# Encoder queries: the exponential clipped on GpSimd, the map fed from PSUM, no lifted copy on ScalarE

## The reference

```python
def _phi(t):
    return jax.nn.elu(t) + 1.0
# for each of 8 layers, for each sequence h [256, 128]:
#   q, k = _phi(h @ Wq + bq), _phi(h @ Wk + bk);  v = h @ Wv + bv
#   linear attention with 16 heads: state = k^T v per head, att = (q state) / (q sum(k) + 1e-6)
#   h1 = LN(h + att @ Wo + bo);  h = LN(h1 + gelu(h1 @ W1 + c1) @ W2 + c2)
```

## Time and profile before

| | us |
|---|---|
| median of three runs | 2956.65 (2946.87 to 2959.39) |
| the profiled execution | 2955.58 |
| its span in the trace | 2954.2 |
| TensorE busy | 2508.7 (85%) |
| VectorE busy | 2083.3 (71%) |
| ScalarE busy | 1787.4 (61%) |
| GpSimd busy | 1189.5 (40%) |

### The profile page before, as it was taken

How to read it: one execution, slowest core, us unless ns; L and a number is a source line. 1 busy time by engine, 2 the same in 40 slices (tenths; PEclk the granted TensorE clock), 3 DMA queues, 4 the chain that set the end, 5 groups by cost and what they waited for, 6 DMA issues and landing times.

```text
span 2954.2 us, 67889 instructions
## 1 busy us (share of the span) xinstructions
PE 2508.7 (85%) x25429; PEld 1981.5 (67%) x25429; DVE 2083.3 (71%) x7733; ACT 1787.4 (61%) x3496; POOL 1189.5 (40%) x1634
## 2 busy tenths in 40 slices
PE   7799998768599769459689999999999998895886
PEld 4467775446477547336479899999988996563555
DVE  6667765873377844664378888888888888546877
ACT  5444445434255334336369999999989996563553
POOL 4200002575623557565542332322234433556413
PEclk9899998979799879679789999999999999997997
DMA  9910000014300024225300000000010100441001
GB/s 233 279 43 3 3 3 1 9 47 137 91 26 26 30 76 137 80 87 160 108 19 16 19 21 14 21 14 14 14 34 23 37 23 8 127 153 36 24 3 30
DMA packets 149543, 164.59 MB, mean 56 GB/s; under 512 B 15713, under 2 KB 123874, under 8 KB 149218
## 3 DMA queue, kind: packets, MB, share of 16 engines
q1 hardware_dynamic: 120770, 85.53, 10.9%
q0 software_dynamic: 28448, 74.71, 8.2%
HBM read 85.18 MB, written 75.01 MB: 54 GB/s over the span
## 4 chain that ended last, share of the span: by engine, by line
PE 38%; DVE 13%; POOL 4%; issue 3%; ACT 1%; DMA 1%; DVEq 0%; POOLq 0%; ACTq 0%
PE banks L3570 6%; PE banks L3555 6%; PE banks L3500 3%; POOL bins L3212 2%; PE banks L3517 2%; PE banks L3536 2%; PE banks L3509 2%; PE banks L3493 1%; PE banks L3535 1%; PE banks L3247 1%; PE banks L3258 1%; PE banks L3260 1%; PE banks L3248 1%; PE banks L3249 1%; PE banks L3526 1%
## 5 line engine op out<-in xcount | busy, mean ns | idle before, releaser
L3671 POOL TENSOR_SCALAR shared_floats<-shared_floats 128x2 f32<-128x2 f32 x256 | 57.7, 225 | 582.7 <-DVE shared_floats L3662 579.0
L3570 PE MATMUL banks<-layer,shared_floats 128*128 128x128 f32 x2048 | 292.0, 275 | 0.0
L3570 PEld LDWEIGHTS banks<-layer,shared_floats 128*128 128x128 f32 x2048 | 258.8, 192 | 0.0
L3555 PE MATMUL banks<-shared_floats,layer 128*128 128x256 f32 x1024 | 243.9, 381 | 0.0
L3960 ACT ACTIVATE shared_floats<-banks,layer 128x256 f32<-128x256 f32 x512 | 210.3, 471 | 51.0 <-PE banks L3555 51.0
L3555 PEld LDWEIGHTS banks<-shared_floats,layer 128*128 128x128 f32 x1024 | 185.9, 192 | 20.2
L3673 POOL TENSOR_TENSOR shared_floats<-shared_floats,neg_half 128x2 f32<-128x2 f32 x256 | 183.7, 717 | 21.3
L1395 POOL DMA_INDIRECT results<-shared_floats,e_token_rows x160 | 155.3, 971 | 89.4 <-issue 48.2
L3683 DVE TENSOR_SCALAR shared_floats<-banks,shared_floats 128x128 f32<-128x128 f32 x512 | 185.4, 403 | 7.3 <-POOL shared_floats L3673 7.3
L2164 DVE TENSOR_REDUCE shared_floats<-banks 128x2 f32<-128x512 f32 (+3 forms) x256 | 110.5, 484 | 91.2 <-PE banks L2028 89.7
L256 PE MATMUL banks<-ident,xn 128*128 128x128 f32 x320 | 60.4, 320 | 133.4 <-issue 82.3
(11 more groups left out here) (444 smaller groups left out, 7939.3 us busy)
## 6 DMA issues: line engine op xcount, KB each, us to landing
bins<-zero SPq DMA_DIRECT2D x1, 18176.0 KB, 69.3
layer<-in_dram_layers SPq DMA_DIRECT2D x16, 902.0 KB, 4.6
bins<-layer SPq DMA_DIRECT2D x16, 650.0 KB, 13.2
shared_floats<-bins SPq DMA_DIRECT2D x32, 325.0 KB, 3.5
expert_weights<-in_dram_experts SPq DMA_DIRECT2D x32, 312.0 KB, 3.1
results<-results SPq DMA_DIRECT2D x32, 256.0 KB, 3.3
results<-zero SPq DMA_DIRECT2D x1, 4096.0 KB, 16.1
bins<-xn,f_bin_row POOLq DMA_INDIRECT x256, 2.3
```

Source lines behind the costliest of these rows:

```text
L3555: m = T.matmul(k.bank[5 + half][:, part], w["w1"][:, tile(n)], h1[:, :], start=True, stop=True)
L3570: m = T.matmul(to, hidden[:, n * S + t * P:n * S + (t + 1) * P], w["w2"][:, tile(n)], start=False, stop=(n == NF - 1), skip_group_check=True)
```

## The change

ScalarE no longer makes the lifted copy (lift_q, e2_q_plus). Its exponential of the queries, exps_q, takes over the waits. GpSimd gets a new instruction per unit, clip_q, which takes the smaller of the exponential and 1 in place, and which stands first in GpSimd's step. VectorE's map_q now reads bank 0, adds (bias + 1) and takes the larger of that and the clipped exponential; it waits for GpSimd. map_k comes before map_q now, and map_q carries the semaphore e2_qk, so that it stands for both. As bank 0 is now read until the end of map_q, TensorE's waits before bank 0 is written again (project_q and all the extra work) are on e2_qk, not on the exponential. In the second half of narrow one product stands ahead of turn_att and three behind it, where it was two and two.

```diff
@@ project_q, and leave in the same way
         if u:
-            T.wait_ge(k.sem("e2_exp_q"), u)
+            T.wait_ge(k.sem("e2_qk"), u)
         T.matmul(k.bank[0][:, LOW], w["wq"], h, start=True, stop=True).then_inc(k.sem("e2_q_made"), 1)
@@ TensorE's step
-            narrow(g - 3, 1, 0, NF // 2)
+            narrow(g - 3, 1, 0, 1)
         if 1 <= g <= U2:
             turn_att(g - 1)
         if g in TURNING:
-            T.wait_ge(k.sem("e2_exp_q"), g + 1)
+            T.wait_ge(k.sem("e2_qk"), g + 1)
             ln_turn(k, s, TURNING[g])
...
         if s.next and (g in ROWS_TURN_AT or g in GATES_AT or g in COUNT_AT):
-            T.wait_ge(k.sem("e2_exp_q"), g + 1)
+            T.wait_ge(k.sem("e2_qk"), g + 1)
...
-            narrow(g - 3, 1, NF // 2, NF)
+            narrow(g - 3, 1, 1, NF)
@@ VectorE
     def map_q(u):
-        q, exp_q, q1 = (k.sb(n, [P, S]) for n in (f"e2_q{u % 2}", "e2_exp_q", "e2_q_plus"))
-        V.wait_ge(k.sem("e2_exp_q"), u + 1)
-        v.count(V.scalar_tensor_tensor(out=q[:, :], in0=exp_q[:, :], scalar=1.0, in1=q1[:, :], op0=ALU.min, op1=ALU.max))
+        q, exp_q = k.sb(f"e2_q{u % 2}", [P, S]), k.sb("e2_exp_q", [P, S])
+        V.wait_ge(k.sem("e2_clipped"), u + 1)
+        V.scalar_tensor_tensor(out=q[:, :], in0=k.bank[0][:, LOW], scalar=layer_weights(k, u)["bq1"], in1=exp_q[:, :],
+                               op0=ALU.add, op1=ALU.max).then_inc(k.sem("e2_qk"), 1)
...
         if g < U2:
+            map_k(g)
             map_q(g)
-            map_k(g)
@@ ScalarE
-    def lift_q(u):
-        w, q1 = layer_weights(k, u), k.sb("e2_q_plus", [P, S])
...
-        a.count(A.activation(q1[:, :], k.bank[0][:, LOW], ACT.Identity, bias=w["bq1"]))
...
-        A.activation(exp_q[:, :], k.bank[0][:, LOW], ACT.Exp, bias=w["bq"]).then_inc(k.sem("e2_exp_q"), 1)
+        A.activation(exp_q[:, :], k.bank[0][:, LOW], ACT.Exp, bias=w["bq"]).then_inc(k.sem("e2_exps"), 1)
@@ GpSimd
+    def clip_q(u):
+        exp_q = k.sb("e2_exp_q", [P, S])
+        G.wait_ge(k.sem("e2_exps"), 2 * u + 1)
+        G.tensor_scalar(exp_q[:, :], exp_q[:, :], 1.0, None, ALU.min).then_inc(k.sem("e2_clipped"), 1)
...
     for g in range(STEPS2):
+        if g < U2:
+            clip_q(g)
         if TURNING.get(g + 1, NC) not in (*ONE_BY_ONE, NC):
```

## The result

The changed kernel takes **2987.0 us** (median of four runs, 2983.8 to 2990.3) where the kernel before takes 2955.2 in the same comparison: a ratio of 1.0115, 95% interval 1.0097 to 1.0132, so 1.15% slower. The forecast was 2975 and the range 2952 to 2992. The profiled execution is 2983.84 us, its span 2982.4, which is 28.2 above the span before.

What follows compares the result with a forecast made beforehand. TensorE was taken to bound the encoder's long middle, VectorE and in places GpSimd's queue its ends. 2955.6 - 13.4 (plain steps) + 1 (VectorE-limited steps) + 18.9 (bank 0 waits) + 6.5 + 6.4 (queue) = 2975 us; range 2952 to 2992.

Steps and rivals of the forecast that it cites:

- The plain step: Encoder steps without extra turning, TensorE-limited: attention copy 0.16 us sooner, 7.52 to 7.36; 84 steps, 13.4 us gained (0 to 17.6).
- The clip: GpSimd's new instruction on 128x256 in SBUF: 0.40 us taken, bounds 0.31 and 0.76, plus 0.05 for the wait.
- if the clip takes over 0.65, as it then delays every step: Sign against the forecast: a GpSimd clip longer than 0.65 us would delay all steps.
- Part 2: Clip of 0.40 us covered in plain steps, 0.25 to spare before VectorE asks; 1 us lost for all VectorE-limited steps.
- The waits for bank 0: Steps using bank 0 for extra work: TensorE now waits for VectorE's queries' map; 27 x 0.70 = 18.9 us lost (13 to 23).
- turning step: Encoder step in which TensorE also transposes a residual chunk, such as step 29: 8.4 us forecast instead of 7.73.
- GpSimd's queue: Clip behind queued gathers, scatters and roots: 6.5 us lost at the start, 6.4 in steps 88, 96, 104 and 112.
- Part 4: Pricing of clips late in GpSimd's in-order queue: steps 0 and 1 lose 6.5 us, four late steps 1.6 each.
- The turning waits are empty: Rival: TensorE meets no wait for VectorE's queries' map in steps turning a chunk; 2956 us, not slower; chance 0.20.
- the plain steps gain nothing: Rival: in steps without extra turning, slight lateness of VectorE's division eats the gain; 2989 us; chance 0.14.
- The queue does not bite: Rival: no loss from GpSimd's queue, bank 0 waits cost 0.35 each, whole 0.21 gained; 2947 us, faster; chance 0.09.
- the second rival: Same as "the plain steps gain nothing": 2989 us in the text, chance 0.14.

## Why the prediction was right, and where it was off

The direction, the places of the main terms and their signs were right, and 2987 lies inside the range; the sum was 12 too low by the medians, and by its own terms 14 (33.6 against 19.4), of which 5.4 is hidden again, by chance, by the stretch outside the encoder. The largest error was the price of the clip, and one place of loss was missed.

- **The plain step: right in mechanism, 0.06 short in size.** Forecast 7.36, measured 7.30; the whole 0.21 went. "From there ScalarE runs without a gap to the attention copy" was the weak step: copy_att needn't wait for the full 0.55 of copy_h1; it starts 0.45 to 0.48 behind copy_h1's start when its input is there. That the two edits only work together was argued there and is shown by the four kernels: a plain step falls by nothing with the copy left out, by 0.11 with the product moved and by 0.22 with both. The number of plain steps was 84 in the text; 67 gained the 0.22 from widening to widening (63 by the mark of the table, which hides the gain of 30, 46 and 62 and some others in the step ahead of each). That the sums come out alike, 13.4 forecast and 13.6 or 14.7 measured, is luck: the count was too high and the gain per step too low. Of the other 17, six (25, 27, 41, 43, 57, 59) come behind steps in which VectorE has spare work between map_q and the statistics (24, 26 and so on); there the clip comes too late, and they rose by 0.08 to 0.18 instead of falling. With the clip of 0.55 us they fell by 0.04 to 0.11. 26 and 119 gained less, 0.15 and 0.09. 83, 91, 99, 107 and 115 gained 0.13 to 0.14; that the mark shows them 1.14 longer is its fault again, as by the widenings the wait for bank 0 lies in 82, 90 and so on, 1.05 each, where the text had put it. 78, 79 and 80 rose, by 0.21, 0.93 and 0.10, and 23, 9.12 long before, stayed.
- **The clip: the mis-sized term.** 0.40 taken, 0.76 as the upper end, 0.87 measured. Both nearest rows were too cheap a guide: the copy of 128x512 in rows 6 takes 611 ns, and an operation of one input and half the columns takes 260 ns more. By one of its own signs the prediction would be wrong: "if the clip takes over 0.65, as it then delays every step". That sign did not hold: at 0.87 the 67 plain steps still gained their 0.22, and a clip that ends 1.46 behind its start costs a plain step 0.24. The 0.65 is the 0.40 and the 0.25 to spare before VectorE asks; Part 2 itself had the statistics behind map_q wait for TensorE for another 0.22, and the sign left that room out.
- **The waits for bank 0: right in mechanism, too small with the clip.** Priced 0.70, so that a turning step would take 8.4; from widening to widening step 29 took 8.85, 1.12 more than before, and most of the late borrowing steps lost 1.00 to 1.06. The 0.90 by the mark of the table has the gain of step 30 in it. By the clip of 128 columns 0.34 of the 1.12 is the clip's length, and 0.78 stays with a shorter clip, as map_q comes last on VectorE and its end, not the exponential's, releases TensorE. So the 0.70 was near for the clip it was worked out with, and the 0.85 for a clip of 0.76 was some 0.15 too low (1.12 less the 0.11 by which that clip is shorter). In eight late steps (85, 89 and every four to 113) 0.22 to 0.24 of the loss is the moved product, which the kernel with neither copy nor clip loses too; the text had it in its price for step 89, 0.50 + 0.22.
- **GpSimd's queue: right in place, too small.** VectorE's wait in step 0 was to be 6 us and was 7.10; in step 1 it was to be 6 again and was 1.79. Part 4's own sum does not give 6 there: it has VectorE 4.85 late already when the map of step 1 comes 6.3 late, which leaves about 1.5 of wait. In step 88 it was 3.26 where 2.5 was forecast; the 0.47 by which the clip is longer makes most of that. Missed altogether were five clips (steps 78, 86, 94, 102, 110) that stand behind the 1.04 us root of a leaving chunk; the steps behind them (79, 87, 95, 103, 111) lost 0.9 each. What Part 4 lists ahead of the clip are gathers, scatters and the roots of entering or sent chunks; the leaving chunks' root, leave_rstd (L4000 after), is not among them. Here it is in step 86:

```profile
2144.77 1.04 POOL L4000 TENSOR_TENSOR shared_floats<-shared_floats,neg_half 128x4 f32<-128x4 f32 x1
2145.89 1.11 POOL L4005 TENSOR_SCALAR shared_floats<-shared_floats 128x256 f32<-128x256 f32 x1
...
2145.87 0.41 DVE L3742 SCALAR_TENSOR_TENSOR shared_floats<-shared_floats 128x256 f32<-128x256 f32 x1
2147.03 0.48 DVE L3735 SCALAR_TENSOR_TENSOR shared_floats<-banks,layer,shared_floats 128x256 f32<-128x256 f32 x1 [0.75 <-POOL shared_floats L4005]
```

- **The rivals.** *The turning waits are empty* and *the plain steps gain nothing* both fell, by 0.78 us of TensorE's idle time in step 29 and by the 7.30 of the plain steps. *The queue does not bite* fell too, as the queue was worth 17 us, but its third condition, that the whole 0.21 is gained, came true. The sum of the second rival is 2988 by the text's own terms, not 2989.

What stays open: a fill for the hole of 0.78 was not tried, with the three products ahead of the borrowed work.

## What to carry to other kernels

Before a value is left in a shared buffer for a later reader, list every step in which somebody else borrows that buffer, and price the borrower's wait by the end of the new reader, not by that of the old one. An operation handed to an idle engine is put into that engine's queue: list all that stands ahead of it there, arithmetic as well as DMA issues, step by step. Where an operation has two inputs that come together, one edit alone shows nothing or only a part, and where an edit gains in some steps and loses in others, the trace names the steps, and the program can take either way in each.

## What the runs showed of the hardware

GpSimd's clip in place takes 376 ns for 64 columns, 537 for 128 and 856 for 256 (medians; 228 for the 2 columns of L3671, another TENSOR_SCALAR): about 2.5 ns for each column past a start of some 0.22 us. VectorE does the same 256 columns in 0.28 us. A copy of 128x512 on GpSimd (611 ns, rows 6) is no guide to this.

The length was not VectorE's doing: at 1478.64 VectorE stood idle, and the clip took 0.87. In six steps, however, it took 1.10 or 1.11. In each of these VectorE's map_k, with two inputs in SBUF, had started 0.02 to 0.04 ahead of it, as at 2145.87 above; with the longer clip, where map_k is 0.11 ahead, it took 1.01. Both fit a clip that is held until 0.26 to 0.28 behind map_k's start. Where the clip starts first, by 0.34 us in a plain step, neither is held: 0.86 and 0.43. Where it is 0.20 ahead (four steps), map_k takes 0.49 instead of 0.42, and in step 3, where it is 0.11 ahead, 0.57.

The Trainium skill (SBUF — State Buffer, "SBUF: two separate sides") has the first of such a pair hold the shared port for its whole instruction. The trace agrees that the later one is held, and differs in how long: 0.26 to 0.28 behind the start of the first, and not for the 0.86 of a clip. In plain steps the keys' map, 0.34 behind the clip's start, takes 0.43, so the 2 us which that rule would have put there are not there.
